# Last attention of a four-layer gated model: rough scores begun two groups ahead, side products regrouped

## The reference, cut to what matters

```python
def _L3_xattn_ref(x, latents, ...):
    H, Dh = (8, 64)
    xn = layer_norm(x, ln_media_w, ln_media_b)
    zn = layer_norm(latents, ln_lat_w, ln_lat_b)
    q = (zn @ Wq).reshape(b, Nz, H, Dh).transpose(0, 2, 1, 3)
    kv_in = jnp.concatenate([xn, zn], axis=1)
    k = (kv_in @ Wk).reshape(b, F, H, Dh).transpose(0, 2, 1, 3)
    v = (kv_in @ Wv).reshape(b, F, H, Dh).transpose(0, 2, 1, 3)
    sim = jnp.einsum('bhqd,bhfd->bhqf', q * scale, k)
    alphas = jax.nn.softmax(sim, axis=-1)
    out = jnp.einsum('bhqf,bhfd->bhqd', alphas, v)
    return out.transpose(0, 2, 1, 3).reshape(b, Nz, H * Dh) @ Wout
```

## Time and profile before

| | before |
|---|---|
| median of the runs | 1903.68 us |
| the profiled execution's own time | 1899.88 us |
| its span, first to last instruction | 1897.9 us |
| TensorE busy | 1632.0 us, 86% of the span |
| VectorE busy | 1071.7 us, 56% |
| ScalarE busy | 898.0 us, 47% |
| GpSimd busy | 837.5 us, 44% |
| mean granted TensorE clock | 0.925 of full speed |

### The profile page before, as it was taken

The page is one execution under the profiler, slowest core; times in us unless marked ns, Lnnn a source line. Parts: engine busy times, 40 slices in busy tenths (PEclk is TensorE's granted clock), DMA queues, the critical chain, the costliest instruction groups (busy, mean ns, idle before and its releaser), DMA issues.

```text
span 1897.9 us, 26172 instructions
## 1 busy us (share of the span) xinstructions
PE 1632.0 (86%) x9225; PEld 1112.9 (59%) x9225; DVE 1071.7 (56%) x2202; ACT 898.0 (47%) x1454; POOL 837.5 (44%) x754
## 2 busy tenths in 40 slices
PE   5953999969966899965996987999999999997998
PEld 3443999946744333355994665555555655563774
DVE  4761556567967355542546698555555656544335
ACT  2422445413335898823442664555555355431363
POOL 3053211223469454422005474566665666754106
PEclk9776999979987899977998997899999999997999
DMA  9613233030000000062113000000000000012354
GB/s 359 235 46 121 80 136 133 24 119 1 1 22 1 1 7 6 7 279 87 46 48 108 1 1 34 1 0 1 1 0 1 1 0 1 0 69 81 123 167 133
DMA packets 61878, 117.74 MB, mean 62 GB/s; under 512 B 7247, under 2 KB 50499, under 8 KB 59064
## 3 DMA queue, kind: packets, MB, share of 16 engines
q1 hardware_dynamic: 53688, 95.90, 14.4%
q0 software_dynamic: 8064, 20.19, 3.2%
HBM read 72.26 MB, written 44.89 MB: 62 GB/s over the span
## 4 chain that ended last, share of the span: by engine, by line
PE 67%; DVE 12%; POOL 8%; issue 4%; DMA 4%; ACT 4%; SPq 0%; POOLq 0%; DVEq 0%; ACTq 0%
PE psum L166 62%; DMA arena<-xb 2%; POOL arena L1839 2%; POOL arena L870 2%; DVE rounded L2330 2%; DVE arena L1736 1%; POOL xb L1057 1%; POOL arena L1856 1%; DVE arena L171 1%; DVE arena L2401 1%; PE psum L682 1%; DVE arena L1968 1%; ACT arena L1607 1%; DVE arena L187 1%; PE psum L206 1%
## 5 line engine op out<-in xcount | busy, mean ns | idle before, releaser
L166 PE MATMUL psum<-arena 128*128 (+16 forms) x5084 | 1025.5, 435 | 115.8 <-DVE arena L1717 18.8
L166 PEld LDWEIGHTS psum<-arena 128*128 128x128 f32 (+4 forms) x5084 | 586.2, 174 | 450.0 <-issue 287.2
L166 PE MATMUL psum<-rounded 128*128 128x256 f32 (+9 forms) x3072 | 531.0, 338 | 6.0 <-ACT rounded L1572 1.4
L166 PEld LDWEIGHTS psum<-rounded 128*128 128x128 f32 (+5 forms) x3072 | 403.5, 185 | 141.2 <-issue 54.6
L2500 POOL TENSOR_TENSOR arena<-arena 128x1024 f32<-128x1024 f32 (+1 forms) x111 | 263.5, 2374 | 128.7 <-ACT arena L2450 124.8
L2401 DVE TENSOR_REDUCE arena<-psum 128x1 f32<-128x512 f32 x256 | 163.7, 682 | 97.0 <-PE psum L166 95.4
L2450 ACT ACTIVATE arena<-psum 128x1024 f32<-128x1024 f32 x144 | 147.4, 1025 | 145.1 <-PE psum L166 144.4
L1607 ACT ACTIVATE arena<-psum,arena 128x1024 f32<-128x1024 f32 x128 | 134.6, 1117 | 20.5 <-PE psum L166 19.2
L870 POOL DMA_INDIRECT arena<-yb,arena x48 | 46.0, 959 | 210.9 <-DMA yb<-arena 197.4
L1210 POOL DMA_INDIRECT yt<-arena x40 | 39.9, 998 | 183.3 <-DVE arena L1173 177.8
L918 DVE SCALAR_TENSOR_TENSOR rounded<-arena,rounded 128x540 fp32r<-128x540 f32 (+1 forms) x96 | 81.8, 885 | 33.4 <-ACT rounded L1119 32.3
(11 more groups left out here) (265 smaller groups left out, 1905.0 us busy)
## 6 DMA issues: line engine op xcount, KB each, us to landing
arena<-in_w SPq DMA_DIRECT2D x8, 2048.0 KB, 9.1
arena<-xb SPq DMA_DIRECT2D x70, 128.0 KB, 2.3
yb<-arena SPq DMA_DIRECT2D x70, 128.0 KB, 1.8
arena<-in_w1u SPq DMA_DIRECT2D x4, 2048.0 KB, 14.5
xb<-arena SPq DMA_DIRECT2D x3, 2048.0 KB, 16.0
xb<-arena SPq DMA_DIRECT2D x2, 2064.0 KB, 32.2
arena<-xb SPq DMA_DIRECT2D x8, 516.0 KB
yt<-arena SPq DMA_DIRECT2D x2, 2048.0 KB, 15.6
```

Source lines behind the costliest of these rows:

```text
L166: return e.matmul(o, l, r, start=start, stop=stop, skip_group_check=True)
```

## The change

- Each group's rough scores are in the order 1 to 16 and then the latents' (0), for all groups; before, group 0 alone had that order.
- They begin earlier: of group G + 2 two in step 7 and two in step 8; of group G + 1 two in each of steps 0 to 5 and the latents' alone in step 6. So step 6 has one product, and steps 7 and 8 have two of the next group. Before the loop four products of group 1 are made instead of one.
- The joined maxima of group G + 1 move from step 8 to step 7 on VectorE. The first reduction of a group waits until the maxima of the group before are made (`s_mx`).
- The queries' side product "q" moves from step 1 to step 0. The last third of keys or values moves from step 5 to step 6, but not in groups 8 and 9.
- The first rough product of a group waits for the second third of the keys only; the latents' product waits for the last third.

```diff
-            if j == 1 and G + 2 < 16:
+            if j == 0 and G + 2 < 16:
                 return ("q", G + 2, 0)
-            if j in (2, 4, 5) and n + 1 < 8:
-                return ("v" if G % 2 else "k", n + 1, (2, 4, 5).index(j))
+            last = 5 if G in (8, 9) else 6
+            if j in (2, 4, last) and n + 1 < 8:
+                return ("v" if G % 2 else "k", n + 1, (2, 4, last).index(j))
...
-        def rough_order3(G):
-            return list(range(17)) if G else [*range(1, 17), 0]
-
-        def rough_step3(j):
-
-            return [0] if j == 8 else [2 * j + 1, 2 * j + 2]
+        ROUGH_ORDER3 = [*range(1, 17), 0]
+
+        def rough_at3(G, j):
+
+            H, k = (G + 2, 2 * j - 14) if j >= 7 else (G + 1, 2 * j + 4)
+            return [(H, r) for r in ROUGH_ORDER3[k:k + 2]] if H < 16 else []
...
             if at % 17 == 0:
                 e.wait_ge(s_lo3, SIDE3_LOW["q", G, 0])
-                e.wait_ge(s_mo, SIDE3_KEPT["k", n, 1 if G == 0 else 2])
+                e.wait_ge(s_mo, SIDE3_KEPT["k", n, 1])
...
             if i == 0:
-                if G == 0:
-                    e.wait_ge(s_mo, SIDE3_KEPT["k", 0, 2])
+                e.wait_ge(s_mo, SIDE3_KEPT["k", n, 2])
...
         def dve_rough3(e, G, i):
             bk, at = rough3(G, i)
             e.wait_ge(s_am, at + 1)
+            if G and at % 17 == 0:
+                e.wait_ge(s_mx, 48 + G)
...
             pe_side3(e, FIRST3[8])
-            pe_rough3(e, 1, 0)
+            for r in ROUGH_ORDER3[:4]:
+                pe_rough3(e, 1, r)
...
                     if side3(G, j):
                         pe_side3(e, side3(G, j))
-                    if j < 8 and G + 1 < 16:
-                        for i in rough_step3(j):
-                            pe_rough3(e, G + 1, i)
-                    if j == 8 and G + 2 < 16:
-                        pe_rough3(e, G + 2, 0)
+                    for r in rough_at3(G, j):
+                        pe_rough3(e, *r)
...
-                    if j == 8 and G + 1 < 16:
+                    if j == 7 and G + 1 < 16:
                         dve_maxima3(e, G + 1)
                     if side3(G, j):
                         dve_side3(e, side3(G, j))
-                    if j == 8 and G + 2 < 16:
-                        dve_rough3(e, G + 2, 0)
-                    if j < 8 and G + 1 < 16:
-                        for i in rough_step3(j):
-                            dve_rough3(e, G + 1, i)
+                    for r in rough_at3(G, j):
+                        dve_rough3(e, *r)
```

More of the change, by code:

```diff
@@ L1978, in dve_mid @@
                         for k in ROUGH_TAKEN[i]:
-                            dve_rough3(e, 0, rough_order3(0)[k])
+                            dve_rough3(e, 0, ROUGH_ORDER3[k])
                 t = i - 6
@@ L2125, in pe_mid @@
                     for k in ROUGH_EARLY[i]:
-                        pe_rough3(e, 0, rough_order3(0)[k])
+                        pe_rough3(e, 0, ROUGH_ORDER3[k])
                 if 17 <= i < 23 and STAGES >= 7:
@@ L2348, in build @@
         ROUGH_TAKEN = {21: (0, 1), 22: (2, 3), 23: (4, 5)}
-        def rough_order3(G):
-            return list(range(17)) if G else [*range(1, 17), 0]
-        def rough_step3(j):
-            return [0] if j == 8 else [2 * j + 1, 2 * j + 2]
+        ROUGH_ORDER3 = [*range(1, 17), 0]
+        def rough_at3(G, j):
+            H, k = (G + 2, 2 * j - 14) if j >= 7 else (G + 1, 2 * j + 4)
+            return [(H, r) for r in ROUGH_ORDER3[k:k + 2]] if H < 16 else []
         def rough3(G, i):
-            k = rough_order3(G).index(i)
+            k = ROUGH_ORDER3.index(i)
             if G == 0:
@@ L2534, in pe_xattn3 @@
             pe_side3(e, FIRST3[7])
-            for r in rough_order3(0)[8:]:
+            for r in ROUGH_ORDER3[8:]:
                 pe_rough3(e, 0, r)
             pe_side3(e, FIRST3[8])
-            pe_rough3(e, 1, 0)
+            for r in ROUGH_ORDER3[:4]:
+                pe_rough3(e, 1, r)
             e.wait_ge(s_mo, SIDE3_KEPT[FIRST3[7]])
@@ L2586, in dve_xattn3 @@
             e.memset(x3_NM, 0.0)
-            for i, r in enumerate(rough_order3(0)[6:]):
+            for i, r in enumerate(ROUGH_ORDER3[6:]):
                 dve_rough3(e, 0, r)
@@ L2592, in dve_xattn3 @@
             dve_side3(e, FIRST3[8])
-            dve_rough3(e, 1, 0)
+            for r in ROUGH_ORDER3[:4]:
+                dve_rough3(e, 1, r)
             for G in range(16):
                 for j in range(9):
-                    if j == 8 and G + 1 < 16:
+                    if j == 7 and G + 1 < 16:
                         dve_maxima3(e, G + 1)
```

## The result

The changed kernel takes 1934.32 us in the median (1933.06 to 1935.23, 4 runs) against 1903.28 us for the kernel before in the same comparison: 1.0163 times as long, 95% interval 1.0151 to 1.0176, or 31 us more. The forecast was 1921.9 us, with a range of 1909 to 1933; the result lies 1.3 us above the range. The direction was right, and so was the exchange of one wait for another; some 13 us more were lost than the sum had, which holds no term for the clock. (By the last call in the reference, the 64 keys that the texts call the latents' are the 64 rows of the context, and the 1024 tokens are the queries and the other 1024 keys; sizes and steps are as described.)

What follows compares the result with a forecast made beforehand. TensorE, busy 86% of the span, was taken to set the pace at 2.4 GHz. Terms 15.4 + 3.0 - 0.5 + 1.5 - 3.2 + 1.5 + 0.5 = +18.2 us on 1903.68 gave 1921.9 us, range 1909 to 1933.

Steps and rivals of the forecast that it cites:

- The queries' product in step 0: Groups 0 to 13: 1.00 us taken from step 2, 2.10 us put into step 1; +15.4 us in all.
- The last third in step 6: "k2" uncovered in six even groups +3.0 us; "v2" in step 6 -0.5; step 5 of odd groups +1.5.
- Step 7: Step 7 loses its wait, about 0.25 us in each of 13 groups: -3.2 us (-1.8 to -4.7).
- Step 0: Third score matmul, which needs "m" read out, perhaps starts without weights at hand: 15 x 0.10 = +1.5 us (0 to +3.0).
- The sum of the order: All terms of the forecast together, loop and begin: +18.2 us, from +5.5 (low ends) to +28.6 (high ends).
- The 0.5 us ahead of the loop: Four rough products before the loop instead of one, less work missing in group 14: +0.5 us (-0.7 to +2.5).
- rival 3: Clock falls to 1.2 GHz after each of 20 long waits (steps 1 and 5): 34 us more, 1956 us; chance 0.06.
- Rivals 1 and 2: 1: waits go, none replaces them, 1876.9 us, chance 0.06; 2: wait moves to step 1, equal size, 1906.5 us, chance 0.08.

## Why the prediction was right in sign and short in size

- **The queries' product in step 0** was read rightly. Step 1 takes 3.48 us; the six short matmuls without a wait are 1.40, so 2.08 are lost (forecast 2.10), and step 2 without half clock takes 3.18 against 4.18 before, 1.00 gained (forecast 1.00).
- **The last third in step 6** too, as far as whole groups tell, in which all terms come together: even groups without their half clock are longer by about 1.5 us (34.72 - 31.62 - 1.61, group 2), where the terms gave 1.45, and group 3 is longer by 0.97, where they gave 1.12. Step 5 of even groups did not change.
- **Step 7** gained 0.17 us a group, not 0.25 (1.65 to 1.48): two short matmuls after the scores still take more than 0.23 each.
- **Step 0** lost the 0.10 us of the sum: it takes 3.30 us, against 3.19 in the kernel before with "q" alone moved, whose rough products have their old order.
- **The sum of the order.** In the loop it was to be some 17.7 us, and it is 16.7: the loop with the wait filled against the loop before. The 0.5 us ahead of the loop cannot be told from what varies there between executions.
- **The failed step is the clock**, a loss that the sum put at nothing and that stood only as rival 3, with a chance of 0.06. The runs showed 17.75 us for it in the loop. The rival's price was near: 1.7 us for each stretch, measured 1.61. Its count was 20 waits, all of them, and 11 had it. What failed is the reason given against it, that group 2 had the wait of step 5 at a clock of 1.00 and that "k2" in it "fills little". Little it is, 0.66 us, but it cuts the wait: TensorE stands still for 0.73 us at a stretch with "k2" in step 5, and for 1.46 without it, as in group 2 of the changed kernel:

```profile
1280.71 2.02 PE L166 MATMUL psum<-rounded 128*128 128x512 f32 x6 [1.46 <-DVE arena L2403]
```

The two runs with the last third moved back and forth bear it out: with "k2" inside the wait no half clock followed step 5; without it, half clock followed in three of six even groups. The wait of the kernel before was not an example of the open wait that the change makes, and so could not speak against the rival.

- **The medians** differ by 31 us and the two profiled loops by 34.45. The loops are those of one execution each, and the other parts vary as well: the span less the loop is 1405.3 us before and 1406.4 in the changed kernel, and from 1401.6 to 1412.9 in all ten profiles, whose kernels differ little there. How the 31 us divide in the other executions is not shown.
- **Rivals 1 and 2** were rightly set low: the wait did not go, and it did not keep its size.

## What to carry to other kernels

When a product is moved ahead so that its readout is no longer waited for, look for the next thing that stands behind that readout on the engine that does it: here the reductions of two other banks. Where two jobs of VectorE free two kinds of banks, put the one first whose bank TensorE asks for first; that order alone was worth some 47 us here, and the moves without it cost 31. And price a wait of the bounding engine twice, once for its length and once for what the clock may do behind it; a wait that looks alike but has a little work in it does not show what the empty one will do.

## What the runs showed of the hardware that was not expected

Behind idle stretches of TensorE of 1.46 us, one or two in a group of some 33 us that is otherwise dense, the granted clock fell to the 1.2 GHz level. In the ten profiled executions, from group 1 on, TensorE stood still 56 times for 1.45 to 1.66 us, and a stretch at that level followed 33 of them; of 78 times for 0.40 to 0.74 us it followed none. One stretch at that level in the changed kernel lies in "v0" of group 1:

```profile
1234.84:1238.25 3.41, 3.41 (x18) 3.41 (x17) 0.00 (x0) 1.04 (x2) 3.27 (x2) 0.50 0.00 0
```

Not every long wait had it: 11 of 20 in the changed kernel's profile, seven of 14 behind step 1 in the kernel before with "q" in step 0, three of six behind step 5 with the last third in step 6. Why one group is taken and the next, with the same steps, is not was not tried and stays open. The Trainium skill (TensorE: Matmul & The Clock Gate, "A second HAM failure mode: psum-queue depth-cycling") tells of short idle times between groups of matmuls that cycle through PSUM banks, after which the clock goes to and fro between its two levels; the traces here agree, with 17.75 us for it in one loop. The other surprise is that matmuls whose results are thrown away made the kernel faster, by 17.75 us of the loop, because they kept TensorE at work where it had to wait anyway.
